# First experts' opening tiles: two experts' low parts of w3 on GpSimd, VectorE's subtractions spread, shares finished first

## The reference, cut to what matters

```
probs = softmax(flat @ Wg); topp, topi = top_k(probs, 2)      # 2048 rows, 8 experts
topp = topp / (sum(topp) + 1e-08)
for e in range(8):
    h = silu(flat @ W1[e]) * (flat @ W3[e])                   # 256 -> 512
    out = out + cw[:, e:e+1] * (h @ W2[e])                    # 512 -> 256, cw from topp
```

## Time and profile before

| | |
|---|---|
| median of three timed runs | 1042.99 us (1041.98 to 1044.61) |
| the profiled execution | 1043.99 us, of which its span 1042.2 us |
| TensorE, matmul | 931.3 us busy (89%) |
| TensorE, weight load | 793.7 us (76%) |
| VectorE | 741.9 us (71%) |
| ScalarE | 616.4 us (59%) |
| GpSimd | 500.5 us (48%) |
| mean granted TensorE clock | 0.955 |

### The profile page before, as it was taken

The page is one execution under the profiler, slowest core; times in us unless marked ns, Lnnn a source line. Parts: engine busy times, 40 slices in busy tenths (PEclk is TensorE's granted clock), DMA queues, the critical chain, the costliest instruction groups (busy, mean ns, idle before and its releaser), DMA issues. The chain is left out here.

```text
span 1042.2 us, 33997 instructions
## 1 busy us (share of the span) xinstructions
PE 931.3 (89%) x12986; PEld 793.7 (76%) x12986; DVE 741.9 (71%) x2163; ACT 616.4 (59%) x1492; POOL 500.5 (48%) x614
## 2 busy tenths in 40 slices
PE   4899999999999789989986489999996349999998
PEld 3588888888888678877864377888885338899997
DVE  6387888887878775646665897677764767778874
ACT  2678878788788353344554865566663625455442
POOL 1354444444444323456652277777774034644543
PEclk9999999999999999999997599999998659999999
DMA  6111311311311169600005123333332467654501
GB/s 170 51 51 51 91 51 51 90 51 51 91 50 52 43 160 330 234 3 4 5 4 122 57 37 51 52 51 57 52 54 34 150 198 250 181 131 118 127 7 11
DMA packets 72011, 89.17 MB, mean 86 GB/s; under 512 B 24380, under 2 KB 51536, under 8 KB 71856
## 3 DMA queue, kind: packets, MB, share of 16 engines
q1 hardware_dynamic: 55824, 66.42, 20.8%
q0 software_dynamic: 16032, 20.62, 12.0%
HBM read 67.28 MB, written 21.99 MB: 86 GB/s over the span
## 5 line engine op out<-in xcount | busy, mean ns | idle before, releaser
L132 POOL TENSOR_TENSOR xa_cs<-xa_ctx,xa_cs 128x514 fp32r<-128x514 f32 x64 | 82.7, 1293 | 163.2 <-ACT xa_cs L655 161.8
L1918 POOL DMA_INDIRECT e_x<-rows,source x71 | 76.8, 1082 | 101.5 <-ACTq L1755 34.3
L661 ACT ACTIVATE xa_pr<-xa_pr,xa_nm 128x257 f32<-128x257 f32 x256 | 108.6, 499 | 2.5 <-DVE xa_nm L705 2.5
L709 DVE TENSOR_SCALAR xa_pT<-xa_ptp 128x512 f32<-128x512 f32 x128 | 88.1, 688 | 29.4 <-PE xa_ptp L524 29.4
L698 DVE TENSOR_SCALAR_CACHE_REDUCE xa_pr<-banks 128x257 f32<-128x257 f32 x256 | 93.6, 422 | 19.8 <-PE banks L514 18.8
L2597 ACT ACTIVATE e_h<-e_hb,rc_F_b 128x512 f32<-128x512 f32 x64 | 44.0, 688 | 88.4 <-PE e_hb L2543 88.4
L2543 PE MATMUL e_hb<-e_xTs,e_w1s 128*128 128x512 f32 x384 | 92.3, 401 | 1.9 <-issue 1.9
L1929 POOL DMA_INDIRECT out_x<-e_y,target x32 | 54.1, 1691 | 73.9 <-DVE e_y L2706 61.6
L2559 PE MATMUL e_yb<-e_w2s,e_hTs 128*128 128x256 f32 x768 | 89.5, 278 | 0.0
L1923 POOL DMA_INDIRECT base<-e_y,place x39 | 70.1, 1797 | 38.5 <-DVE e_y L2201 23.6
L2559 PEld LDWEIGHTS e_yb<-e_w2s,e_hTs 128*128 128x128 f32 x768 | 88.2, 188 | 0.1
(11 more groups left out here) (360 smaller groups left out, 2661.8 us busy)
## 6 DMA issues: line engine op xcount, KB each, us to landing
e_w<-in_F_W SPq DMA_DIRECT2D x16, 1024.0 KB, 9.4
w<-in_W SPq DMA_DIRECT2D x24, 512.0 KB, 10.2
xa_ctx<-in_ctxT SPq DMA_DIRECT2D x32, 257.0 KB, 2.9
xa_ctx<-in_ctxT SPq DMA_DIRECT2D x64, 128.5 KB, 3.1
rows<-xs_oT SPq DMA_DIRECT2D x4, 516.0 KB, 9.7
xs_oT<-in_x SPq DMA_DIRECT2D x4, 512.0 KB, 5.4
xa_vb<-vlx SPq DMA_DIRECT2D x64, 32.0 KB
base<-xs_oT SPq DMA_DIRECT2D x4, 512.0 KB, 2.6
```

Source lines behind the costliest of these rows:

```text
L132: pool.tensor_tensor(o["cs"][:, par, 1, :, 0:S], o["ctx"][:, slot, :, par, :], o["cs"][:, par, 0, :, 0:S], ALU.subtract).then_inc(o["cr_re ...
L661: act.activation(pr[:, par, g, :], pr[:, par, g, :], ACT.Exp, bias=nm[:, par, g:g + 1], scale=-1.0).then_inc(exp_ready, 1)
L709: dve.tensor_scalar(pT[:, par, 2 * h:2 * h + 2].rearrange("p g t c -> p (g t c)"), ptp[:], 1.0, None, ALU.min).then_inc(pT_ready, 1)
L1918: return pool.indirect_dma_start(out=out, out_offset=None, in_=rows, in_offset=bass.IndirectOffsetOnAxis(ap=index, axis=0))
```

## The change

It has five parts.

1. The low parts of w3 for experts 2 and 3 move from VectorE to GpSimd (`BY_POOL`, `rest_w3`, semaphore `w3p_ready`). The first stands at the start of GpSimd's part of the phase, the second behind its gather of the rows of tile 2 and ahead of its wait for the shares.
2. The other low parts are put into `AFTER_H` and `AFTER_W2`: at most one behind the product and one behind w2 of a tile.
3. ScalarE's high parts of experts 6 and 7 stand one behind each of tiles 0 to 3 (`HIGH1`, `HIGH3`) instead of two behind tiles 0 and 1.
4. `finish_shares` and the low part of tile 0's rows move ahead of the low part of w3 of expert 0.
5. In the routing block the three instructions of `te` move from before the source list to the block's end on VectorE.

The diff, without the lines of `te` (they are cut and pasted as they are):

```diff
@@ -1955,9 +1954,11 @@
 
 
 EARLY = 3
-HIGH = {0: (6,), 1: (7,)}
-REST1 = {0: (3,), 1: (4,), 2: (5,), 3: (6,), 4: (7,)}
-REST3 = {0: (2, 3), 1: (4,), 2: (5,), 3: (6,), 5: (7,)}
+HIGH1 = {0: 6, 2: 7}
+HIGH3 = {1: 6, 3: 7}
+AFTER_H = {0: (1, 3), 1: (1, 4), 2: (3, 4), 3: (1, 5), 4: (1, 6), 5: (3, 6), 6: (3, 7)}
+AFTER_W2 = {3: (3, 5), 5: (1, 7)}
+BY_POOL = (2, 3)
 
 
 def first_experts_phase(nc, rc, rows, base, shares, source, target, place_of, te, b, weight, lg, ws):
@@ -1997,6 +1998,7 @@
         xh_ready = p.sem("e1_xh_ready")
         xl_ready = p.sem("e1_xl_ready")
         w1l_ready = p.sem("e1_w1l_ready")
+        w3p_ready = p.sem("e1_w3p_ready")
         w2h_ready = p.sem("e1_w2h_ready")
         w2l_ready = p.sem("e1_w2l_ready")
         a_ready = p.sem("e1_a_ready")
@@ -2033,10 +2035,18 @@
                     pool.wait_ge(share_loaded[j % 2], 16 * (j // 2))
                 gather_rows(pool, share[:, j:j + 1], shares, target[:, j:j + 1]).then_inc(share_loaded[j % 2], 16)
 
+            def rest_w3(e):
+                pool.wait_ge(b["w3h_ready"], e + 1)
+                pool.tensor_tensor(w13l[:, 4 * e + 2:4 * e + 4, :], w13[:, 4 * e + 2:4 * e + 4, :], b["w3h"][:, 2 * e:2 * e + 2, :],
+                                   ALU.subtract).then_inc(w3p_ready, 1)
+
+            rest_w3(BY_POOL[0])
             for j in range(J1 + 1):
                 if j + 2 < J1:
                     pool.wait_ge(t_ready, j + 1)
                     gather_rows(pool, x[:, j % 2, :], rows, source[:, j + 2:j + 3]).then_inc(x_loaded[j % 2], 16)
+                if j == 0:
+                    rest_w3(BY_POOL[1])
                 if j == 0:
                     pool.wait_ge(shares_written, 16)
                     fetch_share(0)
@@ -2093,7 +2103,10 @@
                 if there(j, 0):
                     pe.wait_ge(h_ready, j)
                     if static(j) and j < E:
-                        pe.wait_ge(w3l_ready, j + 1)
+                        if j in BY_POOL:
+                            pe.wait_ge(w3p_ready, BY_POOL.index(j) + 1)
+                        else:
+                            pe.wait_ge(w3l_ready, j + 1 - sum(e < j for e in BY_POOL))
                     hidden(bb, par, w3h, w13l, (e * 2, e * 4 + 2)).then_inc(b_ready, 1)
                 if there(j, 1):
                     pe.wait_ge(hh_ready, j)
@@ -2140,10 +2153,10 @@
                     act.wait_ge(h_ready, j)
                     act.activation(s[:], ab[:], ACT.Silu).then_inc(s_ready, 1)
                     high_w2(j, par)
-                if static(j):
-                    for e in HIGH.get(j, ()):
-                        high_w1_of(act, b, e)
-                        high_w3_of(act, b, e)
+                if static(j) and j in HIGH1:
+                    high_w1_of(act, b, HIGH1[j])
+                if static(j) and j in HIGH3:
+                    high_w3_of(act, b, HIGH3[j])
 
             high_w1_of(act, b, 3)
             high_w3_of(act, b, 3)
@@ -2190,9 +2203,8 @@
                     if not static(j) or j >= 1:
                         dve.wait_ge(ht_ready, j)
                     dve.tensor_tensor(h[:], bb[:], s[:], ALU.mult).then_inc(h_ready, 1)
-                if static(j):
-                    for e in REST1.get(j, ()):
-                        rest_w1(e)
+                if static(j) and j in AFTER_H:
+                    rest(*AFTER_H[j])
                 if there(j, 1):
                     dve.wait_ge(yb_ready, j)
                     dve.wait_ge(share_loaded[1 - par], ((j - 1) // 2 + 1) * 16 if static(j) else j * 8 + (0 if par == 0 else 8))
@@ -2202,15 +2214,20 @@
                                              op0=ALU.mult, op1=ALU.mult).then_inc(y_ready, 1)
                 if there(j, 0):
                     rest_w2(j, par)
-                if static(j):
-                    for e in REST3.get(j, ()):
-                        rest_w3_of(dve, b, e)
+                if static(j) and j in AFTER_W2:
+                    rest(*AFTER_W2[j])
+
+            def rest(n, e):
+                if n == 1:
+                    rest_w1(e)
+                else:
+                    rest_w3_of(dve, b, e)
 
             rest_w1(0)
+            finish_shares()
+            rest_x(0, 0)
             rest_w3_of(dve, b, 0)
-            rest_x(0, 0)
             rest_w1(1)
-            finish_shares()
             rest_w3_of(dve, b, 1)
             rest_w1(2)
             tiles(dve, step, 1)
```

More of the change, by code:

```diff
@@ L1885, in _ @@
                                   place[:, part].unsqueeze(2).to_broadcast([P, T // 2, P]), ALU.is_equal).then_inc(at_ready, 1)
-            if not capped:
-                link(dve.tensor_tensor(ge[:], tiles[0:1, 0:J1].unsqueeze(2).to_broadcast([1, J1, E]),
-                                       tb[0:1, :].unsqueeze(1).to_broadcast([1, J1, E]), ALU.is_ge))
-                link(dve.tensor_reduce(tef[:], ge[:], AXX, ALU.add))
-                link(dve.tensor_scalar(te[:], tef[:], float(E - 1), None, ALU.min))
             dve.wait_ge(inv_ready, 1)
@@ L1914, in _ @@
                 link(dve.tensor_scalar(place_of[:], place_of[:], 1, None, ALU.arith_shift_right))
+                link(dve.tensor_tensor(ge[:], tiles[0:1, 0:J1].unsqueeze(2).to_broadcast([1, J1, E]),
+                                       tb[0:1, :].unsqueeze(1).to_broadcast([1, J1, E]), ALU.is_ge))
+                link(dve.tensor_reduce(tef[:], ge[:], AXX, ALU.add))
+                link(dve.tensor_scalar(te[:], tef[:], float(E - 1), None, ALU.min))
 def gather_rows(pool, out, rows, index):
```

## The result

The changed kernel took 1048.95 us (median of 20 runs) beside 1044.72 us (20 runs) of the kernel before on the same chip. The ratio is 1.0045, with a 95% interval from 1.0032 to 1.0058: slower, by 4.7 us (3.3 to 6.1). The forecast was 1045.0 us, +2.0, "within 0.3%" as the likeliest. One of the runs of the kernel before took 1095.79 us and is left out of the ratio. The sign was right, the size was half; the time lies 0.95 us above the stated range (1038.5 to 1048). Of the 3.95 us by which the time itself was missed, 1.73 are the level (the kernel before took 1044.72 us here and 1042.99 when it was first timed), and the rest is the change's price.

The account below looks back on a forecast made before the run. The opening was bound by TensorE waiting for VectorE's low parts, with GpSimd backlogged. Later phase +0.9, waits behind GpSimd +3.0, back by tile 2 -1.9, after it 0.0: +2.0 on 1042.99 gives 1045.0 us, range 1038.5 to 1048.

Parts of the forecast that it names:

- The list's move: End of the routing block on VectorE: the phase opens 0.9 us later, bounds +0.6 and +1.2 us.
- GpSimd's price: Each 128x1024 subtraction on GpSimd takes 2.42 us, twice what VectorE needs (1.22).
- The exclusion: VectorE instructions with two SBUF inputs and GpSimd instructions reading SBUF don't overlap: the later waits for the other's end.
- Rival 1: The two engines' subtractions overlap in the opening: time 1039.5 us, between 1037 and 1041.5; chance 0.27.
- The other way round as well: GpSimd, when second to come, also waits for VectorE's instruction to end, as with the adds.
- the order in which they meet: Phase's opening: VectorE's w1 goes first, GpSimd's first subtraction waits, its second meets w3; tile 0 +2.0, tile 1 +3.9 us.
- the signs given for "right": Opening: among others, one VectorE subtraction of 3.5 us instead of 1.22 and a shares' instruction of about 2 us.
- What comes back by tile 2: Between tiles 1 and 2: 1.9 of the 3.9 us lost return, through two removed subtractions less the colder clock.
- After tile 2: Tiles after tile 2: 0.0 us together, ends -1.1 (both tiles' gain) and +1.6 (GpSimd's lateness).
- rival 2: GpSimd's backlog lasts longer, tiles from 12 on still 5.5 us apart: +4.5 us taken, 1047.5; chance 0.18.
- Rival 3: GpSimd's backlog clears sooner, half of 5.6 us lost over tiles 2 to 12 returns: -0.8, 1042.2 us; chance 0.10.
- a colder clock in the main case: A tenth of the main case (chance 0.45, range 1043.2 to 1046.5), counted towards slower than 1046.1 us.

Follow-up runs that it names:

- the pair of kernels that only write or only read: Changed kernel with GpSimd's two subtractions back on VectorE, plus two useless GpSimd memsets or subtractions; untimed, last instruction at 463.4 (writes) and 467.6 us (reads).
- the five kernels with two of them: Changed kernel, its repeat, it with the list back, kernel before with only GpSimd's two, and useless GpSimd reads; last instruction at 467.3 us in the mean.
- GpSimd's first alone: Changed kernel with only expert 2's subtraction on GpSimd, expert 3's back on VectorE after w2 of tile 1; 1046.53 us, 1.001 of the kernel before.
- the five kernels without the reading subtractions: Kernel before, its repeat, it with only the list moved, changed kernel with GpSimd's two back, and GpSimd writes only; last instruction at 463.6 us in the mean.
- the eleven kernels and repeats of the table above: Traces of both kernels, their repeats and seven variants, timed from VectorE's L1880; last instruction between 461.5 and 467.6 us.
- the three kernels that gather ahead of the add: Row gather ahead of the add in the kernel before (0.9978), in the changed kernel (1.0003), and with all subtractions on VectorE and the old list place (0.9962).
- only GpSimd's two: Kernel before with only the w3 low parts of experts 2 and 3 moved to GpSimd; 1.004 of the kernel before.
- after, list back: Changed kernel with the list's three instructions back before the source list; 1.004 of the kernel before.
- the kernel with the memsets: Changed kernel with GpSimd's two subtractions back on VectorE and two GpSimd memsets in their places; not timed, last instruction at 463.4 us.

## Why the prediction went wrong, step by step

**The list's move: right.** +0.9 us forecast, the phase opens 1.05 us later (10.81 - 9.76), with the same 0.61 us behind the last instruction. Only it wasn't worth its face value: beside a GpSimd subtraction 0.3 us at tile 0, alone nothing at the end.

**GpSimd's price: right.** 2.42 us estimated, 2.35 and 2.37 measured.

**The exclusion: right for VectorE, and shown by the pair of kernels that only write or only read.** Rival 1, in which the engines overlap, is out. "The other way round as well" is not borne out for GpSimd's subtractions: in the five kernels with two of them none takes more than 2.49 us, where 2.34 is the shortest.

**The step that failed** is the order in which they meet: "GpSimd wants its first subtraction at about the same time, waits until 589.97 and holds until 592.4", and then "It gets 594.75 to 597.2". Counted from the start of L1880 in each execution (578.10 and 579.47), so that the two can be compared:

| | forecast | measured |
|---|---|---|
| w1 of expert 0 on VectorE | 10.65 to 11.87 | 10.81 to 14.23 |
| GpSimd's first | 11.87 to 14.30 | 10.80 to 13.15 |
| GpSimd's second | 16.65 to 19.1 | 15.09 to 17.46 |
| low part of tile 0's rows | 15.2 to 15.6 | 18.33 to 18.75 |
| tile 0 on TensorE | 15.7 | 18.90 |

It was GpSimd that had the first turn. It did not wait, so its gather and its second subtraction came earlier, the second by 1.6 us, and VectorE's w1 ended later. The second subtraction therefore caught VectorE among the shares' instructions, ahead of tile 0's rows, instead of at the w3 of expert 0 behind them. Both waits then stood before tile 0: it is +5.2 over before and not +2.0. Tile 1 is +5.6, not +3.9. What the first subtraction alone costs there (1.51 us, paid back by tile 2) is near to what I had for it (2.0 less 0.9 for the list, 1.1). The missed term is the second: I had 1.9 us for it, at tile 1, all of it back by tile 2; it measured 2.85 at tile 0 and 3.2 at tiles 1 and 2 (24.59 - 21.38, 30.03 - 26.81), and nothing of it came back. Two of the signs given for "right" came, one subtraction of 3.5 us (3.42) and a long instruction of the shares ("about 2 us", 3.04), but from other meetings than the ones named: the 3.5 was meant for w3 of expert 0, and the shares were to meet the first subtraction, not the second. One clue was passed over: the prediction counted only the shares' instructions "of which three read two SBUF tensors" as exposed, and what was caught is a TENSOR_SCALAR with a single SBUF input. The Trainium skill has it, on the page "SBUF — State Buffer" in the same section and on "VectorE: DVE Perf Modes", section "Mode 2×_2P — use both read ports for one tensor": such an instruction can use both read ports for one tensor, and then contends too. The trace agrees that it is held: 0.17 us became 3.04; that it used both ports here no run shows. That is the smaller part of the miss, since in the kernel with GpSimd's first alone the low part of tile 0's rows starts at 15.48 on the same clock, after 15.09: the second subtraction would have met it, or the shares' product of two SBUF tensors at 15.18, anyway.

**What comes back by tile 2.** I forecast 1.9 us. The step from tile 1 to tile 2 takes 5.44 us (30.03 - 24.59), against 6.7 forecast, since TensorE's clock was full from tile 1 on (0.62 us for what I had at half speed), and so tile 2 stands at 30.03, beside 29.7 forecast. Two errors cancelled. But the kernel before was measured in an execution with a half-speed down projection. Over the five kernels without the reading subtractions tile 2 comes at 25.9 to 28.4, 27.0 in the mean, not 27.62; over the five with them at 29.9. The difference is 2.9 us, where 2.0 was forecast.

**After tile 2: 0 forecast, +0.8 measured** (3.70 at the last instruction less 2.86), within the ends given (-1.1 and +1.6). By stretches of the same means it is 0.2 up to tile 12, 0.5 from there to tile 38, and 0.2 behind: no place stands out, and the traces of one kernel differ by as much. GpSimd fetches its first shares 2.4 us later than before (20.14 on this clock beside 17.70), where the prediction had 1.6. The long steps are not chance, though. In the eleven kernels and repeats of the table above a step of 5.9 to 6.7 us stands behind tile 31 in ten, behind tile 18 in eight and behind tile 11 in five, with and without the change, and in none of the three kernels that gather ahead of the add. In the changed kernel one is this, on TensorE between tiles 18 and 19:

```profile
695.14 0.60 PE L2099 MATMUL e_hb<-rc_ident,e_h 128*128 128x128 f32 x4
697.14 0.44 PE L2075 MATMUL e_tb<-rc_ident,e_x 128*128 128x128 f32 x2 [1.39 <-DMA e_x<-rows,source]
```

Rows that come late, as rival 2 has it; but the kernels without the subtractions have such steps as well, and its test (tiles 5.5 us apart from 12 on) isn't met: 133.8 us for those 26 tiles, 5.15 each, beside 130.7 and 132.4 in the two traces of before. Rival 3 is out likewise: tiles 2 to 12 take 53.5 us, 5.35 each, and kernels with the change spread over 53.5 to 55.3, those without over 53.1 to 55.2.

**The chances.** A loss of over 0.3% had 0.26, 0.17 of it from rival 2 and the rest from a colder clock in the main case. The result has that size by another way, which had no case of its own, so that its size agrees with rival 2's +4.5 is chance: both waits before tile 0. The prediction said that the order of the two engines decides, took one order, and put its own range at 1046.5, without an end for the other.

## What to carry to other kernels

A subtraction given to GpSimd is not taken off VectorE when both read SBUF: here it was VectorE that stood still for GpSimd's 2.35 us, at twice VectorE's own price for the work. Before such a move, look at which chain the stretched instruction stands in, price both orders of arrival, and take the worse as an end of the range. A delay of the first tile is not the price: of the two that fell there, one (1.51 us) was back after two tiles and the other (2.85 us) never was. Why they differ no run shows. And run the kernel before more than once, from a mark close to the change: the one execution that this sum was made against held 1.2 us of cold matmuls that its repeat did not have.

## What the runs showed of the hardware

**Who comes first can't be read from the records' starts.** In four kernels VectorE's w1 meets GpSimd's first subtraction:

| kernel | VectorE starts | GpSimd starts, ends | VectorE ends |
|---|---|---|---|
| after | 590.28 | 590.27, 592.62 | 593.70 (+1.08) |
| GpSimd's first alone | 593.54 | 593.53, 595.88 | 596.97 (+1.09) |
| only GpSimd's two | 590.26 | 590.97, 593.32 | 594.41 (+1.09) |
| after, list back | 589.93 | 590.63, 593.00 | 594.09 (+1.09) |

Whether GpSimd's record starts with VectorE's or 0.7 us later, VectorE ends 1.09 us after GpSimd, and its whole length alone is 1.22. Had it run until GpSimd's recorded start, it would have ended some 0.6 us sooner in the last two. The TENSOR_SCALAR is alike: started 0.63 us ahead of GpSimd's record, 0.17 us long by itself, held to its end. In these cases a gather is in flight on GpSimd as VectorE's instruction starts, but that alone does not hold VectorE: in the kernel before a gather of shares runs from 597.48 to 598.43, and the subtraction of w1 that starts within it at 597.70 takes 1.22 us.

One meeting goes the other way, in the kernel with only GpSimd's two: VectorE's w3 at 594.33 keeps its 1.21 us although GpSimd's second record starts at 595.27, 0.27 us before its end, and it is GpSimd that takes a little longer (2.49). So neither a hold that always begins 0.6 us before GpSimd's record nor one that always breaks into a running instruction fits all the rows. The cause stays open; what is shown is that the order can't be read from the two records' starts, which is how the prediction read it.

**A memset holds the TENSOR_SCALAR too, a little.** With GpSimd only writing, it took 0.34 us instead of 0.17 and ended (593.59) 0.03 us after the memset (593.56); the two-input subtraction beside the same memset kept its 1.23. One case, so no more than a hint that a GpSimd instruction that only writes can hold this one as well.

**The gather pays as well.** GpSimd's gather of rows takes 1.76 us behind VectorE's stretched w1, and ends 0.84 us after it (594.54, 593.70). It takes 0.96 us in the kernel with the memsets, where VectorE's w1 was over before it began. The gather of shares from 597.48 on in the kernel before takes 0.95: VectorE's subtraction (597.70) started after that gather had.
